# Two consecutive tiles of a guidance stage, interleaved in the order of issue

## What is computed

```python
# layer 0
xn = layernorm(x)
k, v, r = xn @ Wk.T, xn @ Wv.T, sigmoid(xn @ Wr.T)
wkv_t = state + exp(time_first) * k_t * v_t;  state = decay * state + k_t * v_t
s = (r * wkv) @ Wo.T
g = silu((silu(xn @ w_gate.T) * (xn @ w_up.T)) @ w_down.T)      # int8-like weights / 127
x = x + s * g
# layer 1
xn = layernorm(x)
normed = unit(xn[t+1] - xn[t])                                  # difference of neighbours
influence = softmax(2 * cos(normed, guidance)) @ guidance       # 512 guidance vectors
blended = 0.6 * normed + 0.4 * influence
s = weighted mean of blended over the last 8 positions
g = silu(xn @ (ternary(weight) * scale).T)
x = x + s * g
```

## Time and profile before

| | us |
|---|---|
| median of 2 runs | 3045.0 |
| the two runs | 3041.4 and 3048.61 |
| the profiled execution | 3039.43 |
| its span, slowest core (core 2) | 3037.9 |
| spans of the eight cores | 3022.5 to 3037.9 |
| PE busy | 2015.8 (66%) |
| DVE busy | 978.9 (32%) |
| ACT busy | 536.8 (18%) |
| POOL busy | 148.8 (5%) |

### The profile page before, as it was taken

How to read it: one execution, slowest core, us unless ns; L and a number is a source line. 1 busy time by engine, 2 the same in 40 slices (tenths; PEclk the granted TensorE clock), 3 DMA queues, 4 the chain that set the end, 5 groups by cost and what they waited for, 6 DMA issues and landing times.

```text
span 3037.9 us, 24001 instructions; the slowest of 8 cores (3022.5 to 3037.9 us)
## 1 busy us (share of the span) xinstructions
PE 2015.8 (66%) x8759; PEld 887.8 (29%) x8759; DVE 978.9 (32%) x1533; ACT 536.8 (18%) x833; POOL 148.8 (5%) x83
## 2 busy tenths in 40 slices
PE   3774305698448965598556984498656985579754
PEld 1332102343213422233223432143322432134321
DVE  1420232431334222352325313352223523353232
ACT  1110222111121111211121111211121111211121
POOL 0000100000000010000010000000100000100100
PEclk9896657899669986799678996699767996789866
DMA  7998210532023410343005320243003420143100
GB/s 174 206 208 192 78 60 14 179 133 83 7 91 124 153 42 14 125 158 119 1 23 198 111 83 7 104 150 150 6 21 124 160 111 0 48 146 121 73 14 21
DMA packets 64500, 291.39 MB, mean 96 GB/s; under 512 B 2945, under 2 KB 3458, under 8 KB 58242
## 3 DMA queue, kind: packets, MB, share of 16 engines
q1 hardware_dynamic: 50322, 252.10, 22.4%
q0 software_dynamic: 14064, 37.75, 6.8%
HBM read 273.07 MB, written 44.04 MB: 104 GB/s over the span
## 4 chain that ended last, share of the span: by engine, by line
PE 56%; DVE 15%; DMA 13%; issue 6%; ACT 5%; POOL 3%; DVEq 0%; SPq 0%; ACTq 0%; POOLq 0%
PE pa L53 25%; PE pb L53 19%; PE pc L53 8%; DVE argA L53 5%; DVE argC L53 3%; DMA ring<-wk_i 3%; PE pt L53 3%; DMA ring<-wd_i 2%; POOL argA L53 2%; DMA ring<-wuT 2%; DVE stats L53 2%; ACT argA L53 2%; DMA wu_i<-ring 2%; ACT L53 1%; DVE bw L53 1%
## 5 line engine op out<-in xcount | busy, mean ns | idle before, releaser
L53 PE MATMUL pa<-xn0T,ring 128*128 128x512 bf16 x2304 | 576.1, 395 | 113.3 <-DVE argB L53 49.6
L53 PE MATMUL pb<-xn0T,ring 128*128 128x512 bf16 x2304 | 554.7, 384 | 0.0
L53 PEld LDWEIGHTS pa<-xn0T,ring 128*128 128x128 bf16 x2304 | 229.7, 100 | 407.7 <-issue 155.7
L53 PEld LDWEIGHTS pb<-xn0T,ring 128*128 128x128 bf16 x2304 | 229.4, 100 | 285.2 <-issue 23.8
L53 PE MATMUL pt<-identb,xnt 128*128 128x128 bf16 x512 | 64.7, 306 | 367.4 <-DVE xnt L53 367.4
L53 PE MATMUL pa<-ring,argA 128*128 128x512 bf16 x768 | 186.1, 407 | 111.0 <-DMA ring<-wd_i 72.4
L53 ACT ACTIVATE argC<-pa 128x512 bf16<-128x512 f32 (+1 forms) x112 | 73.7, 658 | 912.0 <-PE pa L53 912.0
L53 ACT ACT_TABLE_LOAD x80 | 102.6, 1283 | 699.4 <-PE pc L53 500.3
L53 DVE TENSOR_TENSOR argA<-argC,argB 128x512 bf16<-128x512 bf16 x192 | 81.7, 426 | 266.5 <-ACT argC L53 266.5
L53 PEld LDWEIGHTS pt<-identb,xnt 128*128 128x128 bf16 x512 | 49.5, 137 | 385.3 <-issue 385.3
L53 DVE CAST argB<-pa 128x512 bf16<-128x512 f32 (+1 forms) x112 | 85.9, 767 | 179.6 <-PE pa L53 179.6
(11 more groups left out here) (133 smaller groups left out, 1688.4 us busy)
## 6 DMA issues: line engine op xcount, KB each, us to landing
ring<-wu_i SPq DMA_DIRECT2D x14, 3072.0 KB, 11.0
ring<-wg_i SPq DMA_DIRECT2D x14, 3072.0 KB, 11.0
ring<-wd_i SPq DMA_DIRECT2D x14, 3072.0 KB, 10.0
out<-argA SPq DMA_DIRECT2D x32, 512.0 KB, 2.6
ring<-wk_i SPq DMA_DIRECT2D x7, 2048.0 KB, 13.9
ring<-wv_i SPq DMA_DIRECT2D x7, 2048.0 KB, 18.2
ring<-wr_i SPq DMA_DIRECT2D x7, 2048.0 KB, 7.9
ring<-wo_i SPq DMA_DIRECT2D x7, 2048.0 KB, 7.8
```

Of the source, the lines that this page charges most:

```text
L53: ins = getattr(eng, attr)(*args, **kwargs)
```

## The change

`tile_main` is cut into four functions with the same instructions in them: `tile_dots` (dots, exp, reciprocal and small product), `tile_gw` (transposes, copy, influence), `tile_t2blend` (t2 and blend) and `tile_numf1` (num, f1, g1, tr1, tg, residual, store). A new function `tile_pipeline` calls them for the tiles of a chunk in another order: dots of the next tile stand between t2/blend and num of this one, and the next tile's transposes, copy and influence stand behind this tile's store. The matmuls, their shapes, the buffers and the loads are the same. `dens_batch` was called before the tiles already; the branch that would have called it inside the first tile is gone, and it was never taken.

```diff
-    def tile_main(idx, dcm, x1src, xnTsrc, mmat, use_prev, out_rows, v_stats,
-                  v_rden, bwh_unused):
-        sl = pt_seq[0] % 2
-        bwc, bwh = bw[sl], bw[1 - sl]
+    def tile_dots(idx, dcm, v_stats):
         psum_use("pd")
...
         t_dots = R.bump("t")
-        if v_rden[0] is None:
-            v_rden[0] = dens_batch(n_tiles_now[0], v_stats, mmat is mfirstb)
-        E["scalar"].wait(sem_t, R.val("t"))
+        E["scalar"].wait(sem_t, t_dots)
...
         v_c2r = R.bump("v")
+        return a_exp, v_c2r
+
+    def tile_gw(idx, a_exp):
         E["tensor"].wait(sem_a, a_exp)
...
         buf_set("gwT", sem_t, t_inf)
+        return t_inf
+
+    def tile_t2blend(idx, sl, t_inf, v_c2r):
+        bwc = bw[sl]
         E["vector"].wait(sem_t, t_inf)
...
         buf_set("t2", sem_v, v_bw)
+        return v_bw
+
+    def tile_numf1(idx, sl, dcm, x1src, xnTsrc, mmat, use_prev, out_rows,
+                   v_rden, v_bw):
+        bwc, bwh = bw[sl], bw[1 - sl]
         E["tensor"].wait(sem_v, v_bw)
...
+    def tile_pipeline(tiles, v_stats, v_rden):
+        n = len(tiles)
+        st = {0: tile_dots(0, tiles[0][0], v_stats)}
+        ti = {0: tile_gw(0, st[0][0])}
+        for idx in range(n):
+            sl = pt_seq[0] % 2
+            v_bw = tile_t2blend(idx, sl, ti[idx], st[idx][1])
+            if idx + 1 < n:
+                st[idx + 1] = tile_dots(idx + 1, tiles[idx + 1][0], v_stats)
+            dcm, x1src, xnTsrc, mmat, use_prev, out_rows = tiles[idx]
+            tile_numf1(idx, sl, dcm, x1src, xnTsrc, mmat, use_prev, out_rows,
+                       v_rden, v_bw)
+            if idx + 1 < n:
+                ti[idx + 1] = tile_gw(idx + 1, st[idx + 1][0])
+            pt_seq[0] += 1
...
-        v_rden = [dens_batch(len(tiles), v_stats, c == 0)]
-        for idx, tl in enumerate(tiles):
-            tile_main(idx, tl[0], tl[1], tl[2], tl[3], tl[4], tl[5], v_stats,
-                      v_rden, None)
+        v_rden = dens_batch(len(tiles), v_stats, c == 0)
+        tile_pipeline(tiles, v_stats, v_rden)
```

More of the change, by code:

```diff
@@ L516, in build_fused @@
     pt_seq = [0]
-    n_tiles_now = [0]
     carry_v = {}
@@ L703, in tile_main @@
         psum_set("pc", sem_a, a_g1)
-        E["vector"].wait(sem_v, v_rden[0])
+        E["vector"].wait(sem_v, v_rden)
         E["vector"].wait(sem_t, t_num)
@@ L725, in tile_main @@
         buf_set("tg", sem_st, st_c)
-        pt_seq[0] += 1
+    def tile_pipeline(tiles, v_stats, v_rden):
[13 more added lines that the diff above has]
+            pt_seq[0] += 1
     sq_fc = {}
@@ L980, in build_fused @@
         v_stats = stats_batch(len(tiles))
-        n_tiles_now[0] = len(tiles)
-        v_rden = [dens_batch(len(tiles), v_stats, c == 0)]
-        for idx, tl in enumerate(tiles):
-            tile_main(idx, tl[0], tl[1], tl[2], tl[3], tl[4], tl[5], v_stats,
-                      v_rden, None)
+        v_rden = dens_batch(len(tiles), v_stats, c == 0)
+        tile_pipeline(tiles, v_stats, v_rden)
         E["vector"].wait(sem_v, R.val("v"))
@@ L1012, in build_fused @@
     v_stats = stats_batch(1)
[L1013 to L1016, removed]
+    v_rden = dens_batch(1, v_stats, False)
+    tile_pipeline([(deprev[:], x1prev[:], xn1Tprev[:], mbandb, True,
+                    (NCH - 1) * T + (NT - 1) * 128)], v_stats, v_rden)
     E["sync"].wait(sem_st, R.val("st"))
```

## The result

The changed kernel takes 2984.65 us (median of 11 runs, the lowest 2975.7) against 3047.73 us before (median of 10). The ratio is 0.9802, 95% interval 0.9775 to 0.9828. By the ratio that is 60 us less, by the medians 63; 66 were forecast. Measured again beside the kernel before, the ratio was 0.9777 (0.9754 to 0.9799). The profiled execution of the changed kernel has a span of 2989.9 us on its slowest core, core 5; the eight cores lie between 2963.2 and 2989.9.

A forecast was written before the change was run, and what follows sets the result against it. In the tile stages engines take turns, TensorE's pauses also costing clock; nothing there is memory-bound. Gains of 10.1 (dots leave the leg), 46.1 (clock) and 10.2 (table loads) sum to 66.4 us: 2979 against 3045.0, put at 2978, range 2964 to 3002.

The forecast's parts named there:

- part 1: Leg from f1 to influence: without dots the copy starts earlier, 0.44 us a pair, 10.1 us over 23 pairs.
- part 2: Pause before num: dots fit into its 3.24 us at no cost; at worst 0.2 us a pair, 4 us.
- part 3: Num and f1: with dots shortening the pause, all run at the high clock, 2.0 us a pair, 46.1 us.
- The upper bound: Clock gain in num and f1: 2.0 us a pair if all 20 matmuls always run fast; the lower bound was 0.
- the short pause of layer 0: A 1.47 us TensorE pause in layer 0 that left the clock at 1.00, taken as evidence for the full gain.
- part 4: Queues of ScalarE, VectorE, GpSimd and SyncE: moved instructions hold nothing up; slack 2.0 us for Silu, 2.9 for GpSimd; no cost.
- part 5: ScalarE's Exp and Silu table loads: 80 become 64, and each chunk's last Silu needs none, saving 10.2 us.
- No clock change: Num and f1: the clock rise is still spent in the pause, only parts 1 and 5 remain, 3025 us; chance 0.07.
- Half the gain: Num and f1: half the clock gain, if the rise often comes only after dots, 3002 us; chance 0.12.
- Slower by a clock that falls in the remaining pause: Num and f1 run low throughout, 8.5 us instead of 6.3: 30 us slower, 3075; chance 0.06.
- VectorE slowed by the writes beside it: T2 and blend double while TensorE writes dots, losing 59 of the 66 us: 3038; chance 0.03.
- the case in which every influence runs low: Influence, its leg keeping only transposes, runs all low: 0.19 us a pair, 4 us, 2982; chance 0.3 within the main case.

The follow-up runs named there:

- the repetition: Kernel before, in its own order, with the same tile's 8 dots issued again in the pause before num: 2983.95 us, ratio 0.9803.
- the add behind the blend: Changed kernel with a tile's residual add and store moved behind the next tile's t2 and blend on VectorE: ratio 0.9242, lowest run 2814.41 us.
- 4 repeats: Kernel before with only 4 of the same tile's 8 dots issued again in the pause before num: ratio 0.9919.
- the best order: Changed kernel with residual add and store behind the next tile's t2 and blend: ratio 0.9242; with the last tiles' dots repeated too, 2794.23 us, ratio 0.9172.
- the dots one place off: Changed kernel with the next tile's dots between num and f1, leaving the pause before num empty: 3073.51 us, ratio 1.0064.

## Why the prediction was right

**The sum.** Forecast 66.4 us, from a per-pair gain in three terms and one term per chunk. Measured in the stages:

- *Dots leave the leg (part 1).* 0.44 us a pair forecast, 7.45 - 6.99 = 0.46 measured, 10.6 us. The reading that dots had been covered by the Silu path held: taking them out won nothing but the reciprocal and the small product ahead of the copy.
- *Dots enter the pause (part 2).* Nothing forecast, 6.65 and 6.66 us measured.
- *The clock (part 3).* 2.0 us a pair forecast, 6.28 - 4.32 = 1.96 measured, 45.1 us. The upper bound was the right choice, and the short pause of layer 0 the right row: pauses were 0.95 and 1.45 us in the cycle shown and at most 2.03 in the 184 pairs.
- *What is held up (part 4).* The next Exp ran before this Silu, and Silu started with its load 0.3 us behind f1 (1519.90) as before. No cost.
- *Table loads (part 5).* 64, as forecast; 10.2 us forecast, 9.8 and 10.2 measured by putting one back.

10.6 + 45.1 + about 10 = 66. **The missed term** is the tiles without a next one: "as before" was assumed, but their num and f1 went from 6.19 to 6.52 us, in the eight of the stages 2.6 us lost. Together 63, which is what the stages lost, 63.3. What made these tiles slower I haven't separated; filling their pause removes it with the rest. The overall ratio gives 60, and 63 lies within its interval.

**Layer 0.** It was said to keep its length. The time up to and between the tile stages summed to 2341.4 us before (means of the cores). In the changed kernel's profile it was 2350.6, but in the kernels of the experiments, whose layer 0 is the same, it ranged from 2340.7 (the repetition) to 2353.3 (the add behind the blend), with no tie to the tile stages' length. What stands out in the profile of the changed kernel are stretches with a granted clock of 0.81 (third from last), between the two usual levels, as in the second row, from its slowest core; the first row is the same core a chunk earlier:

```profile
2359.00:2409.00 50.00, 50.00 (x234) 22.65 (x232) 15.45 (x30) 10.15 (x17) 0.00 (x0) 1.00 0.29 106
2710.00:2760.00 50.00, 50.00 (x192) 20.73 (x191) 13.39 (x24) 7.16 (x12) 0.00 (x0) 0.81 0.28 105
```

All four cores of the second die have such stretches, 120 to 167 us in sum, and none of the first; the profile before has none at all. In cores 4 and 5 they fall mostly in the last chunk's layer 0, which took 284.1 and 280.7 us there and 264.6 to 266.5 on the first die. That makes 4 us in the mean of the eight cores, and 14 to 16 on core 5 alone, more than the 5 by which the profiled span, 2989.9, lies over the median. In cores 6 and 7 they fall in the first chunk's layer 0. No experiment says what brings them about.

**The rivals.** No clock change (3025): refuted by f1's mean. Half the gain (3002): it didn't come, as all 184 pairs kept the level; 4 repeats instead of 8 do bring something like it, 25 us. Slower by a clock that falls in the remaining pause: that does happen behind longer pauses, 2.38 us with 4 repeats and 3.24 before, but not behind those of the changed kernel. VectorE slowed by the writes beside it: t2 and the blend take 1.28 us each in the changed kernel's timeline, and in the mean of all its tiles:

```profile
1530.36 1.28 DVE L53 TENSOR_SCALAR argC<-pa,statL 128x1024 bf16<-128x1024 f32 x1 [4.07 <-PE pa L53]
1531.82 1.28 DVE L53 SCALAR_TENSOR_TENSOR bw<-argB,statL,argC 128x1024 bf16<-128x1024 bf16 x1 [0.17 <-DVE argC L53]
```

The 4 us of the case in which every influence runs low didn't come: influence's mean went from 605 to 609 ns, (4 / 255) x 8 x 0.211 x 23 = 0.6 us, and the leg from influence to num stayed at 6.65 and 6.66 us. The share of its matmuls at the low level went from 0.89 to 0.90, not to 1. The rule of the Trainium skill that the prediction named beside it (TensorE: Matmul & The Clock Gate, Part 4: PE-mode transpose), that transposes don't count as PE-busy in the same way, is neither supported nor refuted by that, since influence was nearly always low either way.

**The chances.** The prediction gave 0.56 to a gain of over 2%. The ratio of 0.9802 has 0.98 within its interval, and the second measurement, 0.9777 (0.9754 to 0.9799), lies just beyond: the gain is 2% within what either can tell.

**What the prediction had in hand and didn't use.** It named the cause that holds the leg at 6.94 us, the copy behind the add on VectorE's queue. Moving that add is worth 177 us in the stages, nearly three times the whole change.

## What to carry to other kernels

Price a wait of TensorE twice: once for its length and once for the clock of the matmuls behind it; in this kernel a 3.24 us pause cost another 2 us in the burst after it, and matmuls that shortened it enough, needed or not, won those back (8 did in every tile, 4 in 95 of 256). When a tile's work is interleaved with the next one's, check every in-order queue for an instruction that waits long and has the next tile's first link behind it; here that was a residual add that nobody was waiting for.

## What the runs showed of the hardware that I had not expected

- Useless matmuls paid: 256 more of them made the kernel 60 us faster (ratio 0.9803), and 72 more on top of the best order, 64 of them in the tile stages, another 9 us there.
- Interleaving alone, with the dots one place off, was no gain but slightly slower than no interleaving (ratio 1.0064, 1.0038 to 1.009).
- A granted clock of 0.81, neither of the two usual levels, over 50 us of unbroken matmuls (192 of them), while the same core had run as long a stretch of the chunk before, 2359 to 2409, at 1.00 (234 matmuls).
- With TensorE at the high level throughout, the blend took 1.36 us instead of 1.28 when the residual add followed it without a gap; I didn't look into it.
